# Attention stage of an audio tower: three operations reordered on ScalarE and VectorE, two loop heads placed on a fetch block

## The reference

```python
h = tok(x)                      # stack 8 frames, rms norm, gated projection, rms norm
h = h + attn(layernorm(h))      # the stage of this change
h = h + ffn(layernorm(h))       # base projection plus routed low-rank terms

# attn, 32 heads, 64 plain and 64 rotary dimensions, low-rank keys and values
q = rmsnorm(x @ wq_a.T) @ wq_b.T             # q_nope, q_pe
kv = rmsnorm(ckv) @ wkv_b.T                  # k_nope, v
q_pe, k_pe = rope(q_pe), rope(k_pe)          # x * cos + rotate_half(x) * sin
scores = q_full . k_full * softmax_scale     # causal mask
out = softmax(scores) @ v @ wo.T
```

## Time and profile before

| | before |
|---|---|
| median of 3 runs | 2439.2 us (2436.16 to 2441.24) |
| the profiled execution, its own time | 2439.96 us |
| its span | 2438.3 us |
| busy: TensorE, VectorE, ScalarE, GpSimd | 95%, 74%, 51%, 50% |
| busy in a turn of the attention (82.05 us) | 79.9, 72.9, 75.2, 58.0 us |

### The profile page before, as it was taken

One profiled execution on the slowest core, in us unless ns is written; L12 is line 12 of the kernel. 1 busy time (PEld: TensorE's weight loads), 2 busy tenths in 40 slices (PEclk: granted clock), 3 DMA queues, 4 the chain that ended last, 5 costly groups with the idle time before them and its releaser, 6 DMA issues. The chain is left out here.

```text
span 2438.3 us, 45823 instructions
## 1 busy us (share of the span) xinstructions
PE 2326.4 (95%) x14640; PEld 2038.1 (84%) x14640; DVE 1811.2 (74%) x3542; ACT 1240.9 (51%) x3724; POOL 1218.7 (50%) x1012
## 2 busy tenths in 40 slices
PE   8999999988899979999999999899999998999998
PEld 6888888866577758999999999788888877899998
DVE  8987777776467758989898989655776575777775
ACT  5566554442355549999999999732332223111110
POOL 5667776673023336677767776510676553111110
PEclk9999999999999989999999999899999999999999
DMA  7774567777466740111111112296888988122121
GB/s 247 242 233 147 180 214 255 241 241 273 147 214 229 229 143 17 57 52 47 51 56 51 45 51 68 69 327 195 241 250 238 290 271 270 53 70 70 69 69 52
DMA packets 319400, 382.00 MB, mean 157 GB/s; under 512 B 23680, under 2 KB 227968, under 8 KB 319104
## 3 DMA queue, kind: packets, MB, share of 16 engines
q1 hardware_dynamic: 311472, 352.30, 45.8%
q0 software_dynamic: 7184, 25.69, 2.7%
q10 hardware_dynamic: 576, 2.10, 0.3%
HBM read 297.68 MB, written 81.80 MB: 156 GB/s over the span
## 5 line engine op out<-in xcount | busy, mean ns | idle before, releaser
L1537 ACT ACTIVATE attn_prob<-attn_prob,attn_bias 94x94 f32<-94x94 f32 x1024 | 366.7, 361 | 45.8 <-DVE attn_bias L1613 44.3
L670 DVE TENSOR_TENSOR up_t_lo<-early_raw,up_t_hi 128x512 fp32r<-128x512 f32 (+1 forms) x210 | 221.0, 1056 | 120.1 <-ACT up_t_hi L596 117.8
L538 POOL TENSOR_TENSOR early_raw<-early_raw 128x512 f32<-128x512 f32 (+1 forms) x150 | 231.9, 1551 | 142.5 <-DMA early_raw<-x_f 82.3
L1658 POOL TENSOR_TENSOR attn_prob<-attn_prob,attn_share 94x752 f32<-94x752 f32 x128 | 188.3, 1471 | 177.5 <-DVE attn_share L1621 177.5
L1913 POOL TENSOR_TENSOR early_raw<-early_raw 128x512 f32<-128x512 f32 x120 | 170.2, 1423 | 199.9 <-DMA early_raw<-o_t 199.5
L1963 DVE TENSOR_TENSOR out_t_lo<-early_raw,out_t_hi 128x512 fp32r<-128x512 f32 x168 | 159.6, 954 | 139.5 <-ACT out_t_hi L1927 138.7
L596 ACT ACTIVATE up_t_hi<-early_raw 128x512 fp32r<-128x512 f32 (+1 forms) x210 | 130.4, 622 | 258.2 <-POOL early_raw L538 179.6
L1927 ACT ACTIVATE out_t_hi<-early_raw 128x512 fp32r<-128x512 f32 x168 | 105.0, 631 | 307.6 <-POOL early_raw L1913 155.9
L734 PE MATMUL up_ps<-up_t_lo,early_s_hi 128*128 128x512 f32 (+1 forms) x616 | 241.1, 391 | 12.8 <-DVE up_t_lo L670 12.8
L735 PE MATMUL up_ps<-up_t_hi,early_s_lo 128*128 128x512 f32 (+1 forms) x616 | 239.1, 388 | 0.0
L736 PE MATMUL up_ps<-up_t_hi,early_s_hi 128*128 128x512 f32 (+1 forms) x616 | 238.9, 388 | 0.0
(11 more groups left out here) (267 smaller groups left out, 6628.2 us busy)
## 6 DMA issues: line engine op xcount, KB each, us to landing
early_raw<-o_t SPq DMA_DIRECT2D x288, 256.0 KB, 4.9
early_raw<-x_f SPq DMA_DIRECT2D x240, 256.0 KB, 3.9
shared_ring<-w SPq DMA_DIRECT2D x120, 256.0 KB, 4.0
early_raw<-x_f SPq DMA_DIRECT2D x120, 240.0 KB, 4.0
shared_ring<-wvo SPq DMA_DIRECT2D x96, 256.0 KB, 4.9
o_t<-attn_o_t SPq DMA_DIRECT2D x128, 188.0 KB, 1.9
shared_ring<-wo SPq DMA_DIRECT2D x32, 512.0 KB, 6.7
y<-early_raw POOLq DMA_DIRECT2D x24, 512.0 KB, 3.6
```

The lines of the kernel that those rows point to most:

```text
L538: nc.gpsimd.tensor_tensor(both[n % 2][:, 0:w], a, b, SEVEN[i].op_b).then_inc(both_done, 1)
L670: nc.vector.tensor_tensor(t_lo[s % NT][:, 0:w], src, t_hi[s % NT][:, 0:w], ALU.subtract).then_inc(lo_done, 1)
L1537: last = nc.scalar.activation(prob[u % NPR][0:SEQ, h, part], prob[u % NPR][0:SEQ, h, part], ACT.Exp, bias=bias[u % 2][0:SEQ, n:n + 1], sca ...
L1658: nc.gpsimd.tensor_tensor(p4, p4, share[u % 2][0:SEQ, :].unsqueeze(2).broadcast_to((SEQ, 8, SEQ)), ALU.mult).then_inc(prob_done, 1)
```

## The change

Three edits, all in `attention`:

- ScalarE: the w_hi split moves from between the ps_l copies and prob_t to behind prob_t; `early_hi` moves from behind the exponentials to ahead of them.
- VectorE: the rotary sum q_b moves from between the mask add and the maximum to behind the bias.
- The loops of ScalarE and of VectorE get `at=0`.

```diff
--- before.py
+++ after.py
@@ -1509,15 +1509,6 @@
                     nc.scalar.activation(q_b[u % 2][64:P, :], ps_l[64:P, 0:GT], ACT.Copy).then_inc(latent_done, 1)
                     if first(j, 1):
                         values_and_keys()
-                    for c in range(2):
-                        s = weights_of(k, m, PREP + c)
-                        if s is not None:
-                            p, w, kb = s
-                            if c == 0:
-                                act.wait_ge(w_in[w], 16 * kb + 16)
-                                if not first(p, 2):
-                                    act.wait_ge(latent_made, GROUPS * (p - 1))
-                            nc.scalar.activation(w_hi[w][:, c, :], w_raw[w][:, c, :], ACT.Copy).then_inc(w_hi_done, 1)
                 s = stage(k, m, D_T, U, N)
                 if s is not None:
                     j, u, kb = s
@@ -1526,6 +1517,17 @@
                         act.wait_ge(weighed, j - NPT + 1)
                     nc.scalar.activation(prob_t[u % NPT][0:SEQ, :, :], ps_t[0:SEQ, :, 0:GT],
                                          ACT.Copy).then_inc(prob_t_done, 1)
+                for c in range(2):
+                    s = weights_of(k, m, PREP + c)
+                    if s is not None and stage(k, m, 0, U, N) is not None:
+                        p, w, kb = s
+                        if c == 0:
+                            act.wait_ge(w_in[w], 16 * kb + 16)
+                            if not first(p, 2):
+                                act.wait_ge(latent_made, GROUPS * (p - 1))
+                        nc.scalar.activation(w_hi[w][:, c, :], w_raw[w][:, c, :], ACT.Copy).then_inc(w_hi_done, 1)
+                if early(k, m, 11) is not None:
+                    ow.early_hi(act, early(k, m, 11))
                 s = stage(k, m, D_S, U, N)
                 if s is not None:
                     j, u, kb = s
@@ -1538,11 +1540,9 @@
                                                         bias=bias[u % 2][0:SEQ, n:n + 1], scale=SCALE,
                                                         accum_out=total[u % 2][0:SEQ, n:n + 1])
                     last.then_inc(exp_done, 1)
-                if early(k, m, 11) is not None:
-                    ow.early_hi(act, early(k, m, 11))
 
             act.wait_ge(cleared, NPT)
-            run_steps(act, N, DEPTH, U, body, last=1)
+            run_steps(act, N, DEPTH, U, body, last=1, at=0)
 
         @block.vector
         def _(dve):
@@ -1592,14 +1592,6 @@
                     nc.vector.tensor_tensor(p4, ps_s[0:SEQ, :, 0:GT].rearrange("p h (b k) -> p h b k", b=GB),
                                             mask[0:SEQ, :].unsqueeze(1).unsqueeze(1).broadcast_to((SEQ, 2, GB, SEQ)),
                                             ALU.add).then_inc(masked, 1)
-                s = stage(k, m, 0, U, N)
-                if s is not None:
-                    j, u, kb = s
-                    dve.wait_ge(sin_done, j + 1)
-                    if not first(j, 2):
-                        dve.wait_ge(scored, j - 1)
-                    nc.vector.tensor_tensor(q_b[u % 2][0:64, :], by_cos[0:64, :], by_sin[0:64, :],
-                                            ALU.add).then_inc(rope_b_done, 1)
                 s = stage(k, m, D_S, U, N)
                 if s is not None:
                     j, u, kb = s
@@ -1612,6 +1604,14 @@
                         dve.wait_ge(exp_done, j - 1)
                     nc.vector.tensor_scalar(bias[u % 2][0:SEQ, :], top[0:SEQ, :], -SCALE, None,
                                             ALU.mult).then_inc(bias_done, 1)
+                s = stage(k, m, 0, U, N)
+                if s is not None:
+                    j, u, kb = s
+                    dve.wait_ge(sin_done, j + 1)
+                    if not first(j, 2):
+                        dve.wait_ge(scored, j - 1)
+                    nc.vector.tensor_tensor(q_b[u % 2][0:64, :], by_cos[0:64, :], by_sin[0:64, :],
+                                            ALU.add).then_inc(rope_b_done, 1)
                 s = stage(k, m, D_N, U, N)
                 if s is not None:
                     j, u, kb = s
@@ -1622,7 +1622,7 @@
                 if early(k, m, 12) is not None:
                     ow.early_lo(dve, early(k, m, 12))
 
-            run_steps(dve, N, DEPTH, U, body, last=1)
+            run_steps(dve, N, DEPTH, U, body, last=1, at=0)
 
         @block.gpsimd
         def _(pool):
```

## The result

| | before | after |
|---|---|---|
| median | 2436.16 us (2435.79 to 2441.24, 5 runs) | 2449.19 us (2443.77 to 2454.75, 5 runs) |
| ratio | 1 | 1.0044, 95% interval 1.0031 to 1.0058 |
| one turn in the steady loop | 82.02 us | 83.70 us |
| from the first R of the attention to the R of m14 in the last turn | 645.6 us | 658.4 us |

The change makes the kernel slower: the medians lie 13.0 us (0.53%) apart, and the ratio over all runs is 1.0044. The forecast was 2451 and slower. The profiled execution of after has a span of 2442.1 us, only 3.8 over the one of before, although its attention is 12.7 us longer: the rest of the span, nearly all of it code that was not changed, took 9 us less. Over the profiled executions of all fourteen kernels here this rest takes 1784 to 1800 us.

What follows compares the result with a forecast made beforehand. TensorE was taken as the bound, with about 3.9 us of holes a turn. Steady turns +6.6, first loop turn +2.0, steps ahead +0.5, last steps +0.5, entry +2.1: +11.7, so 2451 us, own range 2444 to 2460.

Steps and rivals of the forecast that it cites:

- turn 0: The 16 attention steps ahead of the loop: an estimated +0.5 us.
- turn 1 with the loop's entry: First turn of the attention loop, +2.0 us, plus a one-time stall on entering the loop, +2.1 us.
- turns 2 to 6: Five attention loop turns behind a back edge, each 16 steps and +1.32 us: together +6.6 us.
- The bias earlier, L's waits gone: VectorE's bias comes 0.35 us earlier, so TensorE's latent products stop waiting for ScalarE's ps_l copy, 3.0 us a turn.
- The scores late by mask start + 2.67: TensorE's odd-step scores wait for the rotary sum, ready 2.67 us after mask-add start: 0.20 us per undisturbed even/odd pair.
- The split steps: Steps where VectorE's weight split, blocked by GpSimd, delays the next scores: two pairs go from 9.97 to 10.96 us.
- (m0,m1): First two of a turn's 16 steps, behind a back edge: 9.97 us against 10.84, so -0.87 us.
- The entry: Entering the aligned attention loop stalls ScalarE and VectorE once: +2.1 us, range 0 to 3.
- ScalarE's moves at nothing: Moving w_hi and early_hi leaves ScalarE's work per step the same: put at nothing, 1 us a turn if cover were gone.
- half the price: Rival, chance 0.19: maximum does not pay the mask add's write-out, 0.05 us per undisturbed pair, 2442 us.
- Faster: Rival, chance 0.13: VectorE's w_lo split starts before GpSimd's normalising, taking 0.42 us, not 1.8; -2.0 us a turn, 2428 us.
- Fetches at every turn: Rival, chance 0.08: an aligned loop head costs 2.85 us idle at each of five back edges, 10.5 us more, 2461 us.

Runs made afterwards that it cites:

- act_only: Kernel before with only ScalarE's two moves (w_hi behind prob_t, early_hi ahead of the exponentials): 2438.81 us, ratio 1.0001 to before.
- slots_only: Kernel before with only both loop heads put on a fetch block (`at=0`): 2436.99 us, ratio 0.9992 to before.
- sum_only: Kernel before with only VectorE's rotary sum moved behind the bias: 2451.92 us, ratio 1.0056 to before.
- split_free_odd: Changed kernel with the rotary sum behind the bias in odd steps only and the w_lo split directly ahead of share: 2417.52 us, ratio 0.9919 to before.
- sum_odd: Changed kernel with the rotary sum behind the bias in odd steps only, in its old place in even ones: 2436.07 us, ratio 0.9990 to before.
- sum_even: Changed kernel with the rotary sum behind the bias in even steps only, in its old place in odd ones: 2447.80 us, ratio 1.0045 to before.
- filler: split_free plus three small unused reciprocals between the bias and the rotary sum: 2441.52 us, turn 81.67 us against 80.14.
- split_free: Changed kernel with VectorE's w_lo split moved to directly ahead of share: 2422.10 us, ratio 0.9929 to before, turn 80.14 us.
- sum_last: Changed kernel with the rotary sum one place further back, behind share: 2437.28 us, ratio 1.0000 to before, turn 81.86 us.
- no_sum: Changed kernel with the rotary sum put back between mask add and maximum: 2436.75 us, ratio 0.9994 to before.

## Why the prediction was right

Term by term, R to R in the two profiled executions:

| part | predicted | measured |
|---|---|---|
| turn 0 | +0.5 | +0.5 (83.11 to 83.63) |
| turn 1 with the loop's entry | +2.0 and +2.1 | +3.4 (81.38 to 84.76) |
| turns 2 to 6 | +6.6 | +8.4 (410.17 to 418.54) |
| turn 7, to m14 | +0.5 | +0.4 (70.98 to 71.42) |
| together | +11.7 | +12.7 |

That 11.7 and 12.7 lie so close is partly luck: the entry was put 1.1 us too high and the steady turns 1.8 too low. The agreement in turn 0 is luck too, since turn 0 takes 83.73 us in act_only and 84.83 in slots_only, where the sum was not moved. And 2451 stands on a median of 2439.2 us from three runs; the five runs of before that are compared with after have 2436.16, so the predicted difference (11.8 us) is a fairer match to the measured 13.0 than the two absolute times.

*The bias earlier, L's waits gone:* right. The waits of after have no line for L; sum_only has the same, so it is the sum that does it. That it is the earlier bias, and not only the longer turn, shows in m1 of split_free_odd.

*The scores late by mask start + 2.67:* right, 2.69 measured. Undisturbed pairs were put at 9.97 us and take 9.95 to 10.07; the one that I took as ordinary and is not is (m2,m3), where the mask add starts 3.79 us after R. sum_odd and sum_even show that it is the even steps' sum, and filler shows that this path has no slack at all.

*The split steps:* right in kind, low in size. (m6,m7) and (m14,m15) were put at 10.96 and take 11.03. split_free shows the cause, and its price.

*(m0,m1):* the largest error inside the turn. I had 9.97 and it takes 10.21. At the end of m0 VectorE is slower than elsewhere: the mask add starts 3.80 us after R for 3.71, the bias 1.06 us behind the maximum for 0.97, and the sum 0.12 behind the bias for 0.08. These add up to the 0.23 us by which m1 is longer than m9 (6.11 for 5.88). Five turns of 0.24 are 1.2 of the 1.8 us that the term of turns 2 to 6 lacked. The back edge is not the cause, for VectorE waits for the rope products there, and sum_only, without the new loop heads, has the same 10.21; what slows these operations no run shows. So the gain of this pair was put down to the wrong part of the change: with the sum moved, the loop heads bring 0.03 us a turn. VectorE's back edge did not become free either, as slots_only shows; the prediction said that both did. Its count for ScalarE's body, 310 instructions and 128 accumulator reads, does not follow from rows 1, whose 310 hold the 128 reads already and no waits; nothing in the sum rests on it.

*The entry:* mechanism right, size too large. VectorE stood for 2.77 us, against 2.85 read from the other loop, but ScalarE hardly:

```profile
989.86 0.55 DVE L1569 TENSOR_TENSOR attn_by_cos<-attn_ps_r,attn_cos 128x376 f32<-128x376 f32 x1 [2.77 <-issue]
...
990.57 0.48 ACT L1508 ACTIVATE attn_q_a<-attn_ps_l 64x376 f32<-64x376 f32 x1 [0.80 <-PE attn_ps_s L1452]
```

I had ScalarE stand for as long, and added the stall to the path. The pair at the entry takes 11.24 us instead of 10.21, so the entry costs 1.0 us and not 2.1.

*ScalarE's moves at nothing:* right within what can be measured (act_only 1.0001). Its turns spread from 82.03 to 82.63 us in one execution, where those of the other kernels repeat within 0.1 in most; why, no run shows.

*The rivals:* "half the price" fell on the 0.03 us between the mask add and the maximum, which is what was measured (1232.31 + 0.92 to 1233.27 is 0.04). "Faster" did not happen in this kernel, since share and the split kept their distance; but its price was right, and sum_last and split_free are that case made. Its condition was too strict: the split need not start before the normalising. In sum_last it came while the normalising was running, 0.23 us from its end, and took 0.51 us. "Fetches at every turn" did not happen.

## What to carry to other kernels

When an operation is moved behind another to let a third start earlier, follow its own result with the same care: write down start to start from the event that releases the chain to the engine that bounds the loop, and compare it with the shortest step of that engine, not with the mean one. Here the mean step of 5.1 us had room for the sum, the even step of 4.1 us had not. And look at each operation whose duration has a long upper side before reordering around it: w_lo's minimum of 0.42 and median of 1.79 us was worth more than the change, and moving it to where the other engine waits anyway took 3.6 us out of every turn.

## What the runs showed of the hardware

- A VectorE operation with two SBUF operands that meets a running GpSimd operation does not simply wait for that one alone. Where VectorE's split came 0.57 us (before, m14) or 0.44 us (sum_last, m13) ahead of the end of GpSimd's operation, GpSimd's next operation went first too, and the split took 1.80 and 1.66 us for 0.41. Where it came 0.23 us ahead of the end, it went in between, and GpSimd's next one waited (1.17 for 0.98). All splits that met the normalising in these kernels fall on these two sides: 0.43 to 0.64 us ahead with 1.65 to 1.87 us, or 0.22 to 0.23 ahead (sixteen in sum_last) with 0.50 to 0.51. The turning point lies between; what sets it is open.
- A loop head on a fetch block took ScalarE's 0.54 us at the back edge away, at every turn of every kernel that has it, and left VectorE's at 0.42 (slots_only, no_sum). Entering the loop stood VectorE still for 2.77 us in after (2.31 to 3.12 in the others) and ScalarE for 0.80 (0.55 to 0.97). What makes the two engines differ was not tried.
- The queue that carries instructions moved fewer packets with the aligned heads: 104 in before, act_only and sum_only, 81 or 82 in the eleven kernels with them. From the pages of before and then after:

```profile
q14 instruction: 104, 0.85, 0.1%
```

```profile
q14 instruction: 81, 0.66, 0.1%
```

The Trainium skill (Runtime: NRT & Kernel Launch, Instruction fetch mechanics) has a taken branch cost a fetch when its target lies outside the two blocks that the engine holds. The 23 packets less, and ScalarE's idle time that went with them, agree. VectorE's idle time is about the same with and without an aligned head (0.42 and 0.37 us), so it need not be a fetch; no run shows what it is.
